# Attention scores as three 64-row products, two heads side by side on the row halves of TensorE

## The reference

```python
b, s, _ = x.shape                                    # 4, 512, 256
q = (x @ Wq).reshape(b, s, 32, 64).transpose(0, 2, 1, 3)
k = (x @ Wk).reshape(b, s, 8, 64).transpose(0, 2, 1, 3)
v = (x @ Wv).reshape(b, s, 8, 64).transpose(0, 2, 1, 3)
q, k = apply_rope(q, pos), apply_rope(k, pos)
k, v = jnp.repeat(k, 4, axis=1), jnp.repeat(v, 4, axis=1)
scores = jnp.einsum('bhqd,bhkd->bhqk', q, k) / 8.0
scores = jnp.where(causal, scores, finfo.min)
out = jnp.einsum('bhqk,bhkd->bhqd', softmax(scores), v)
x = x + out.transpose(0, 2, 1, 3).reshape(b, s, 2048) @ Wo
x = x + int8_linear(layernorm(x))                    # the input of attention is a layernorm too
```

## Time and profile before

| | |
|---|---|
| median of 3 runs | 748.58 us (748.51 to 749.6) |
| the profiled execution | 747.3 us, of which the span from first to last instruction is 745.1 us |
| PE busy | 702.5 us (94%), 8014 products |
| PEld busy | 588.8 us (79%) |
| DVE busy | 658.8 us (88%) |
| ACT busy | 634.4 us (85%) |
| POOL busy | 557.9 us (75%) |
| mean granted clock of PE | 0.992 |

### The profile page before, as it was taken

One profiled execution on the slowest core, in us unless ns is written; L12 is line 12 of the kernel. 1 busy time (PEld: TensorE's weight loads), 2 busy tenths in 40 slices (PEclk: granted clock), 3 DMA queues, 4 the chain that ended last, 5 costly groups with the idle time before them and its releaser, 6 DMA issues.

```text
span 745.1 us, 22980 instructions
## 1 busy us (share of the span) xinstructions
PE 702.5 (94%) x8014; PEld 588.8 (79%) x8014; DVE 658.8 (88%) x1697; ACT 634.4 (85%) x1317; POOL 557.9 (75%) x525
## 2 busy tenths in 40 slices
PE   4889999999999999999999999999999999999993
PEld 3667887878888888888888888888888888888872
DVE  6858999998889989888899898988989988988996
ACT  4778998888889989898889889898898889888883
POOL 4585887787878898787797798778697898777502
PEclk9999999999999999999999999999999999999996
DMA  8233343343334433333333343333433333232300
GB/s 266 57 98 102 73 118 87 83 114 86 87 87 97 85 92 78 87 92 82 86 92 92 94 96 80 87 90 81 96 85 97 87 94 87 67 71 62 86 2 29
DMA packets 56992, 65.80 MB, mean 88 GB/s; under 512 B 12592, under 2 KB 43824, under 8 KB 56880
## 3 DMA queue, kind: packets, MB, share of 16 engines
q1 hardware_dynamic: 53808, 53.85, 30.1%
q0 software_dynamic: 3072, 10.49, 5.1%
HBM read 16.06 MB, written 2.10 MB: 24 GB/s over the span
## 4 chain that ended last, share of the span: by engine, by line
PE 76%; DVE 11%; ACT 8%; issue 3%; DMA 1%; POOL 0%; ACTq 0%; POOLq 0%; DVEq 0%
PE x_bank L644 23%; PE t_bank L788 19%; PE o_bank L807 13%; PE s_bank L767 7%; PE s_bank L768 6%; ACT prob L1098 5%; DVE neg_max L1465 3%; DVE s_bank L1473 2%; PE ot_bank L858 2%; DVE probT L1453 2%; PE s_bank L773 2%; PE t_bank L644 1%; ACT neg_max L1096 1%; DVE value_lo L1323 1%; ACT probT L989 1%
## 5 line engine op out<-in xcount | busy, mean ns | idle before, releaser
L1110 ACT ACTIVATE probT<-t_bank 128x512 f16<-128x512 f32 x320 | 192.1, 600 | 46.3 <-PE t_bank L788 46.3
L1453 DVE SCALAR_TENSOR_TENSOR probT<-t_bank,probT 128x512 f16<-128x512 f32 x320 | 215.2, 686 | 13.5 <-ACT probT L1110 11.4
L788 PE MATMUL t_bank<-ident,prob 128*128 128x128 f32 x1280 | 192.1, 277 | 1.1 <-DVE value_lo L1323 0.7
L1473 DVE CUSTOM_DVE_ANT_0 s_bank<-s_bank,mask_row,score_unit 128x512 f32<-128x512 f32 (+1 forms) x256 | 174.6, 683 | 3.5 <-PE s_bank L768 1.8
L807 PE MATMUL o_bank<-value_hi,probT 128*128 128x65 f16 x2560 | 157.8, 194 | 5.1 <-DVE probT L1453 3.3
L1098 ACT ACTIVATE prob<-s_bank,neg_max 128x512 f32<-128x512 f32 (+1 forms) x256 | 161.2, 645 | 1.2 <-DVE neg_max L1473 1.0
L807 PEld LDWEIGHTS o_bank<-value_hi,probT 128*128 128x128 f16 x2560 | 137.7, 97 | 25.9 <-DVE probT L1453 18.6
L788 PEld LDWEIGHTS t_bank<-ident,prob 128*128 128x128 f32 x1280 | 144.0, 141 | 15.3 <-issue 2.3
L767 PE MATMUL s_bank<-kT,qT 128*128 128x384 f16 (+3 forms) x512 | 140.4, 301 | 11.1 <-ACT prob L1098 7.5
L807 PE MATMUL o_bank<-value_lo,probT 128*128 128x64 f16 x1280 | 141.7, 192 | 0.0
L768 PE MATMUL s_bank<-kT,qT 128*128 128x384 f16 (+3 forms) x512 | 139.3, 299 | 0.0
(11 more groups left out here) (146 smaller groups left out, 1151.3 us busy)
## 6 DMA issues: line engine op xcount, KB each, us to landing
swp<-raw SPq DMA_DIRECT2D x320, 64.0 KB, 2.0
qT<-query_pair SPq DMA_DIRECT2D x256, 64.0 KB, 2.1
kT<-key_pair SPq DMA_DIRECT2D x128, 64.0 KB, 2.0
wg_raw<-in_w_group POOLq DMA_DIRECT2D x16, 384.0 KB, 4.0
wg_raw<-in_w_group POOLq DMA_DIRECT2D x16, 256.0 KB, 3.7
resid<-in_x SPq DMA_DIRECT2D x4, 512.0 KB, 8.4
out<-resid SPq DMA_DIRECT2D x16, 128.0 KB, 1.8
wo_stage<-in_w_out SPq DMA_DIRECT2D x4, 256.0 KB, 3.0
```

The source lines that it names most:

```text
L788: last = nc.tensor.transpose(t_bank[B % TURN_BANKS][:, h * P:(h + 1) * P], prob[:, B % PROBS, h, :], ident[:, :])
L1110: nc.scalar.activation(turned_half[B % TURNED][HI], t_bank[B % TURN_BANKS][:, :], ACT.Copy, scale=PROB_SCALE).then_inc(probT_hi, 1)
L1453: nc.vector.scalar_tensor_tensor(out=turned_half[B % TURNED][LO], in0=t_bank[B % TURN_BANKS][:, :], scalar=PROB_SCALE, in1=turned_half[B % ...
L1473: nc.vector.tensor_tensor_reduce(bank, bank, mask_row[:, SEQ - n:SEQ], score_unit[:, 1, s % KV_HEADS:s % KV_HEADS + 1], UNBOUNDED, ALU.add ...
```

## The change

`scores` no longer takes one group but a pair of groups, in two banks. The 128 rows of `query_pair` are used as they are: one head in rows 0 to 63, the other in rows 64 to 127, and `kT`, which holds the key in both halves, as before. For each pair of heads it makes three products of 64 rows a head, q_hi k_hi, q_hi k_lo and q_lo k_hi, in turn on the upper rows into one bank and on the lower rows into the other; q_lo k_lo is left out. The order of heads in the weights is changed on the host (`SLOT_HEADS`), and the groups become twelve of one or two heads: `v` = 0 now has two groups of two heads, so one more reduction on DVE (L1465), one more scaling of two maxima on ACT (L1096) and one more diagonal product on PE a step. Before a pair PE waits until both its banks are free. `qT`, its semaphores and the 256 DMAs of `place_queries` are gone; `query_pair` has two buffers, and `keep_high` waits for the scores of the step before the last instead. The loops of all five engines are put in a new order.

```diff
-SCORE_GROUPS = ((0, (0, 1, 2, 3)), (1, (0,)), (1, (1,)), (1, (2,)), (1, (3,)),
-                (2, (0,)), (2, (1,)), (2, (2,)), (2, (3,)), (3, (0, 1)), (3, (2, 3)))
+SLOT_HEADS = (0, 2, 1, 3)
+SCORE_GROUPS = ((0, (0, 1)), (0, (2, 3)), (1, (0,)), (1, (2,)), (1, (1,)), (1, (3,)),
+                (2, (0,)), (2, (2,)), (2, (1,)), (2, (3,)), (3, (0, 1)), (3, (2, 3)))
+HALVES = 2
...
-        qT = [sb(f"qT{n}", [P, GROUP_HEADS, SEQ], f16) for n in range(2)]
-        query_pair = sb("query_pair", [P, QUERY_PAIRS, 2, SEQ], f16)
+        query_pair = [sb(f"query_pair{n}", [P, QUERY_PAIRS, 2, SEQ], f16) for n in range(2)]
...
-            def place_queries(s, j):
...
-            def scores(s, a):
+            def scores(s, p):
...
+                for G in range(first, first + HALVES):
+                    if G >= SCORE_BANKS:
+                        pe.wait_ge(exp_done, units_through(G - SCORE_BANKS))
...
-                    for j in range(QUERY_PAIRS):
-                        pe.wait_ge(q_placed[j], s * 64 + 64)
-                for at, h in enumerate(heads):
-                    bank, q = s_bank[G % SCORE_BANKS][:, at * n:(at + 1) * n], qT[s % 2][:, h, i * P:(i + 1) * P]
-                    nc.tensor.matmul(bank, q, kT[s % 2][:, HI, 0:n], start=(at == 0), stop=False, skip_group_check=True)
-                    last = nc.tensor.matmul(bank, q, kT[s % 2][:, LO, 0:n], start=False, stop=(len(heads) == 1),
-                                            skip_group_check=True)
...
+                    pe.wait_ge(lo_kept, tile_no(s, QUERY_PAIRS - 1) + 1)
+                banks = [s_bank[(first + a) % SCORE_BANKS] for a in range(HALVES)]
+                slots = [SCORE_GROUPS[HALVES * p + a][1] for a in range(HALVES)]
+                joint = len(slots[0]) > 1
+                for at in range(len(slots[0])):
+                    j = slots[0][at] % QUERY_PAIRS
+                    for q_part, k_part in ((HI, HI), (HI, LO), (LO, HI)):
+                        for a in range(HALVES):
+                            rows = slice(HEAD_DIM * a, HEAD_DIM * (a + 1))
+                            last = nc.tensor.matmul(banks[a][:, at * n:(at + 1) * n],
+                                                    query_pair[s % 2][rows, j, q_part, i * P:(i + 1) * P],
+                                                    kT[s % 2][rows, k_part, 0:n],
+                                                    start=(at == 0 and (q_part, k_part) == (HI, HI)),
+                                                    stop=(not joint and q_part == LO), skip_group_check=True)
...
+                if joint:
+                    for a in range(HALVES):
...
+                        nc.tensor.matmul(diagonals, ident_b[:, :],
...
@@ keep_high (ACT)
-                if s:
-                    act.wait_ge(q_placed[j], s * 64)
+                if s >= 2:
+                    act.wait_ge(scores_done, group_no(s - 1, 0))
```

More of the change, by code:

```diff
@@ L231, in units_through @@
             s, a = G // len(SCORE_GROUPS), G % len(SCORE_GROUPS)
-            v, heads = SCORE_GROUPS[a]
-            return unit_no(s, v, heads[-1]) + 1
+            return s * UNITS + sum(len(heads) for _, heads in SCORE_GROUPS[:a + 1])
         def inside(s):
@@ new lines, in scores @@
+                slots = [SCORE_GROUPS[HALVES * p + a][1] for a in range(HALVES)]
[10 more added lines that the diff above has]
+                                                    stop=(not joint and q_part == LO), skip_group_check=True)
+                            if not joint and q_part == LO:
+                                last.then_inc(scores_done, 1)
@@ L778, in turn @@
+                if joint:
+                    for a in range(HALVES):
+                        diagonals = banks[a][:, 0:len(slots[a]) * n].rearrange("p (h n) -> p h n", n=n)[:, :, i * P:n]
+                        nc.tensor.matmul(diagonals, ident_b[:, :],
+                                         mask_row[:, SEQ - P:SEQ].unsqueeze(1).broadcast_to([P, len(slots[a]), P]),
+                                         start=False, stop=True, skip_group_check=True).then_inc(scores_done, 1)
             def turn(s, t):
@@ L919, in _ @@
                 project_keys(s + 2)
-                scores(s, 5)
-                scores(s, 6)
-                attend(s, 0)
+                scores(s, 3)
                 turn(s, 1)
                 turn(s, 2)
+                attend(s, 0)
+                out_product(s - 1, 3)
+                scores(s, 4)
                 turn_quant(done_tile(s))
[L926 to L929, removed]
                 turn(s, 3)
                 attend(s, 1)
-                scores(s, 9)
+                turn_output(s, 0)
                 ffn_product(done_tile(s))
+                scores(s, 5)
                 turn(s, 4)
-                attend(s, 2)
-                scores(s, 10)
                 project(s + 2, 0)
                 turn(s, 5)
+                attend(s, 2)
                 attend(s, 3)
+                turn(s, 6)
                 attend(s, 4)
-                turn(s, 6)
                 out_product(s, 0)
+                scores(s + 1, 0)
                 turn_output(s, 1)
+                turn(s, 7)
+                turn(s, 8)
                 attend(s, 5)
-                turn(s, 7)
                 attend(s, 6)
-                turn(s, 8)
                 out_product(s, 1)
@@ L950, in _ @@
                 turn(s, 9)
+                scores(s + 1, 1)
+                turn_output(s, 2)
                 project(s + 2, 1)
-                scores(s + 1, 0)
-                turn_output(s, 2)
-                scores(s + 1, 1)
                 attend(s, 8)
                 attend(s, 9)
+                out_product(s, 2)
                 scores(s + 1, 2)
-                out_product(s, 2)
-                scores(s + 1, 3)
             turn_quant(LOOP_TILES)
@@ L1195, in _ @@
                 exponentials(s, 1, 0)
-                exponentials(s, 1, 1)
-                keep_probT(s, 0)
-                exponentials(s, 1, 2)
                 if s % 2 == 1:
                     keep_wo(s + 1)
+                exponentials(s, 1, 2)
+                keep_probT(s, 0)
+                exponentials(s, 1, 1)
+                exponentials(s, 1, 3)
                 keep_oT(s - 1, 3)
-                exponentials(s, 1, 3)
                 keep_raw_keys(s + 2)
-                keep_high(s + 1, 0)
                 keep_probT(s, 1)
@@ L1223, in _ @@
                 keep_probT(s, 7)
+                keep_probT(s, 8)
+                for h in range(GROUP_HEADS):
+                    exponentials(s + 1, 0, h)
+                keep_high_keys(s + 2)
                 if s % 2 == 1:
                     keep_wo(s + 2)
-                round_tile(done_tile(s + 1))
-                keep_probT(s, 8)
+                keep_probT(s, 9)
+                keep_oT(s, 2)
                 to_whole(done_tile(s + 1))
-                keep_probT(s, 9)
-                keep_high_keys(s + 2)
-                keep_raw(s + 2, 1)
-                keep_oT(s, 2)
                 if s == STEPS - 1:
                     root(2, slice(LOOP_TILES, LOOP_TILES + 2))
-                for h in range(GROUP_HEADS):
-                    exponentials(s + 1, 0, h)
+                keep_raw(s + 2, 1)
             normalise_done(LOOP_TILES + 1)
```

114 lines of the change are left out of this document (52 added, 62 removed).

## The result

| | before | after |
|---|---|---|
| median | 748.55 us | 777.67 us (776.36 to 778.06) |
| ratio | | 1.0385 (1.0367 to 1.0404) |
| span of the profiled execution | 745.1 us | 776.3 us |
| PE busy | 702.5 us | 717.3 us |
| DVE, ACT busy | 658.8, 634.4 us | 664.9, 639.9 us |

The change costs 29.1 us. 758 was forecast, slower, with a range of 720 to 790. The direction is right and the time lies in the range, but the loss is three times the 9 us that the sum gave.

The account below looks back on a forecast made before the run. PE was taken as the bound: 34.9 us of products saved against 44.2 us of switches, other terms 0, gave 9.3 us more, 747.3 to 756.6 for the profiled execution, a median of 758; range 720 to 790.

Parts of the forecast that it names:

- PE is the bound: Whole loop: PE busy 83.60 of 85 us, so its issue time moves the end nearly one for one until DVE binds.
- 34.9 us of products saved: Score products on PE: three product distances in place of four for two heads, 1.09 us saved a step over 32 steps.
- 44.2 us of switches: Edges between full-width and half-array products on PE: 192 excursions at 0.23 us each, at least 32.6 us in all.
- 384 idle times of PEld with "issue": Sign for the forecast: at the edges of excursions, weight loads idle for "issue" about 384 times in the changed profile.
- Weights inside an excursion, 0 and not 17 us: Weight loads of the 18 following pairs a step: taken as hidden, 0; 17 us if exposed, kept for the range.
- DVE and ACT, 15 us hidden: Extra reduction on DVE, 4.8 us, and extra scaling on ACT, 10.2 us, both beside PE's work and so not showing.
- The new order, 0: Reordered loops of all engines: taken as 0, bounded by PE's idle time at about 12 us either way.
- 15 us of changed waits: Sign against the forecast: it falls if PE's waits in the loop change by over 15 us in sum.
- Rival 3: Before the first v = 2 pair in odd steps, PE waits for two free banks: 13 us, total 780; chance 0.16.

Follow-up runs that it names:

- e5: Kernel before plus a 64-row, one-column product ahead of six of ten turns a step, 192 excursions to a row half with nothing gained: 792.66 us.
- e8: Kernel before with one stricter wait: the first group of each pair starts only when two banks are free, products and order untouched: 812.77 us.
- e12: Changed kernel with e1's full-width products, the second v = 1 pair ahead of the third output product and its feeding DVE and ACT steps earlier: 752.59 us.
- e13: e12 without the DMAs that swap the halves of the query projections, output not the reference's: 733.73 us, ratio 0.9804 to before.
- e1: Changed kernel with three full-width products per pair of heads in place of three pairs of 64-row products, scores not the reference's: 753.36 us.
- e6: Kernel before with the same 192 extra one-column products as e5 but on all 128 rows, so no change of the array's partition: 756.19 us.
- e3: Changed kernel with the three upper-row products listed first and the three lower-row ones behind them, for each pair of heads: 778.5 us.

## Why the forecast was right in sign and wrong in size

1. *PE is the bound.* Right, as a limit: e5 turned 192 short stalls of PE into 36.5 us of time, and e8 64.8 us of PE's waits into 64.3. But PE is only the nearest of several chains. In e12's order the next one lies near 752 us (e13), and in the changed kernel's own order e1 stops at 753.36 without a switch, so the full saving of 34.9 us couldn't have shown even with free switches. The forecast put the next bound at DVE's busy time, 8% away, and didn't look at the rotation, which holds no part of the chain but became the bound in e12.
2. *34.9 us of products saved.* Right as a stream: three distances for six products, side by side. As time, e13 shows 14.9 us of it, with 18.9 us of bank waits still in place.
3. *44.2 us of switches.* Right in kind; by e5 and e6 it is 36.5, so 0.19 us and not 0.23 each. Both edges and the load that isn't done ahead are in the rows; the 384 idle times of PEld with "issue" that were to show them are not, since the trace puts the idle time ahead of the score loads down to "issue" only 47 times. The saving per excursion is one product distance for `v` = 1 and 2 (0.22 and 0.16 us) and two for `v` = 3 and 0 (2 x 0.108 and 2 x 0.058), so at 0.19 no excursion gains more than 0.03 us.
4. *Weights inside an excursion, 0 and not 17 us.* Right: inside an excursion pair follows pair at the full-width distance.
5. *DVE and ACT, 15 us hidden.* Nothing speaks against it, though no run takes these instructions away by themselves: over the whole run DVE's busy time rose by 6.1 us and ACT's by 5.5, and both are less busy per stretch than before. The 256-column reduction took 418 ns (0.420 taken), the scaling 298 (0.320).
6. *The new order, 0.* This is the step that failed, and its bounds of 12 us either way with it. They were taken from PE's idle time before, as if an order could only remove or double it. The new waits come from the demand for two free banks out of three: 64 us in the old order (e8), 28.7 - 7.5 = 21.2 us left in the new one. That is also over the 15 us of changed waits at which the prediction said it would fall. Rival 3 had the mechanism and the place; it was given 0.16 and stood apart from the sum, though it belonged in it. Its own price, 0.8 us in 16 odd steps, missed that ACT keeps a turned block ahead of the exponential, which starts at 390.62 though its maximum was through at about 390.30, and the wait in PE is 1.14 us at the step shown. That its 780 lies so near to 777.67 is in part luck: switches that it had 7.7 us too dear and half of 17 us for loads that cost nothing made up for bank waits that it had too cheap.

The sum with the measured terms: - 34.9 + 36.5 + 21.2 + (4.9 - 1.1) for the output products = + 26.6 us, of 29.1. The rest, 2.5 us, isn't assigned. That the sum comes so close is not proof of each term: the terms come from different kernels, and e1 shows that they don't simply add up, since 24.3 and not 36.5 us came back there.

The Trainium skill, "TensorEngine Tiling (Array Packing)", section Restrictions and Gotchas, says that row tiles write to different PSUM banks and so raise the pressure on PSUM. The changed kernel agrees: its row halves need two banks at once, and the bank waits rose by 21.2 us. e8 has no row tiles; it prices the same demand for two banks at 64 us in the old order.

## What to carry to other kernels

Halving the array pays only if an excursion saves more stream than the two switches cost, 0.19 us here; one product distance of 512 columns, 0.22 us, is about break-even. Before a change that takes two buffers at a time, count how far ahead the in-order engine could run with them one at a time: three banks taken singly hid a maximum and an exponential that three banks taken in pairs didn't. And when an engine is 98% busy, ask what would wait next, here the rotation at some 752 us, before a saving is counted in full.

## What was not expected of the hardware

- Products on the two row halves overlap whichever order the program lists them in (e3: 778.5 against 777.7, six products in 0.75 us in both). The third listed product starts fifth in all 128 groups of e3 with 512 or 384 keys.
- One excursion to a row half costs 0.19 us even for a single column (e5, e6), and the weight load isn't done ahead across the switch: in e5 both loads start with their products, at 400.36 and 400.46.
